# Cross-attention on one core: output products of two heads in one visit, with both heads' probabilities transposed first

## What is computed

```python
xn = (input - mu) * rsqrt(var + EPS) * gamma + beta
q  = Wq @ xn + bq                 # 8 heads x 64 channels
k, v = Wkv @ context + bkv
att = softmax(q^T k * 64**-0.5)   # 256 x 256 for each head and sample
y   = att @ v                     # heads concatenated
out = input + Wo @ y + bo
```

## Time and profile before

| | before |
|---|---|
| median of 3 runs | 944.0 us (943.9 to 944.01) |
| span of the profiled execution | 941.7 us |
| TensorE matmul busy | 919.0 us, 98% |
| VectorE busy | 810.3 us, 86% |
| ScalarE busy | 758.3 us, 81% |
| GpSimd busy | 671.0 us, 71% |
| mean granted TensorE clock | 0.999 |

### The profile page before, as it was taken

One profiled execution on the slowest core, in us unless ns is written; L12 is line 12 of the kernel. 1 busy time (PEld: TensorE's weight loads), 2 busy tenths in 40 slices (PEclk: granted clock), 3 DMA queues, 4 the chain that ended last, 5 costly groups with the idle time before them and its releaser, 6 DMA issues.

```text
span 941.7 us, 25082 instructions
## 1 busy us (share of the span) xinstructions
PE 919.0 (98%) x6852; PEld 691.6 (73%) x6852; DVE 810.3 (86%) x1899; ACT 758.3 (81%) x2569; POOL 671.0 (71%) x648
## 2 busy tenths in 40 slices
PE   5999999999999999999999999999999999999998
PEld 4777777777777777777777777777777777777775
DVE  5888889888889888898888898888898888898885
ACT  2788888788888878887888887888888888888785
POOL 2667777667787667877777776677776677777674
PEclk9999999999999999999999999999999999999999
DMA  6444444444444344444444444434444444433431
GB/s 120 100 107 95 114 100 100 96 106 93 107 110 95 91 109 100 95 117 94 95 100 106 100 105 97 104 89 115 103 100 93 106 96 103 114 90 83 96 82 36
DMA packets 72741, 93.32 MB, mean 99 GB/s; under 512 B 15316, under 2 KB 39892, under 8 KB 72724
## 3 DMA queue, kind: packets, MB, share of 16 engines
q1 hardware_dynamic: 70800, 92.72, 42.6%
q10 hardware_dynamic: 1924, 0.40, 0.3%
HBM read 21.76 MB, written 4.19 MB: 28 GB/s over the span
## 4 chain that ended last, share of the span: by engine, by line
PE 53%; DVE 24%; issue 13%; ACT 9%; DMA 0%; DVEq 0%; ACTq 0%; SPq 0%; POOL 0%
PE turned L488 15%; PE out_bank L502 14%; ACT probs L595 8%; PE fill L457 7%; PE fill L458 7%; DVE xhat L722 5%; DVE neg_max L676 5%; DVE probs_t L671 4%; PE misc L518 3%; PE misc L519 3%; DVE c_straight L730 2%; DVE c_crossed L731 2%; PE fill L463 2%; PE fill L464 2%; DVE t_low L687 2%
## 5 line engine op out<-in xcount | busy, mean ns | idle before, releaser
L788 POOL TENSOR_TENSOR probs<-probs,recip 128x512 f32<-128x512 f32 x512 | 526.6, 1055 | 155.6 <-DVE recip L682 150.0
L595 ACT ACTIVATE probs<-fill,neg_max 128x256 f32<-128x256 f32 x1024 | 475.4, 484 | 82.5 <-DVE neg_max L676 82.5
L676 DVE TENSOR_REDUCE neg_max<-fill 128x2 f32<-128x512 f32 x512 | 347.9, 680 | 65.4 <-PE fill L458 60.7
L488 PE MATMUL turned<-ident,probs 128*128 128x128 f32 x2048 | 325.5, 282 | 6.2 <-DVE probs_t L671 6.2
L457 PE MATMUL fill<-c_straight,t_stack 128*128 128x256 f32 x1024 | 308.9, 324 | 0.5 <-DMA t_stack<-t_low 0.5
L488 PEld LDWEIGHTS turned<-ident,probs 128*128 128x128 f32 x2048 | 224.0, 142 | 114.9 <-issue 62.6
L502 PE MATMUL out_bank<-probs_t,values 128*64 128x256 f32 x2048 | 277.5, 392 | 1.4 <-ACT probs_t L586 1.4
L458 PE MATMUL fill<-c_crossed,t_stack 128*128 128x256 f32 x1024 | 265.2, 280 | 0.0
L595 ACT ACTIVATION_READ_ACCUMULATOR probs<-fill,neg_max 128x1 f32 x1024 | 218.8, 214 | 0.0
L586 ACT COPY probs_t<-turned 128x512 f32<-128x512 f32 x256 | 150.1, 586 | 78.2 <-PE turned L488 77.9
L502 PEld LDWEIGHTS out_bank<-probs_t,values 128*64 128x64 f32 x2048 | 124.4, 136 | 105.7 <-issue 34.8
(11 more groups left out here) (61 smaller groups left out, 547.7 us busy)
## 6 DMA issues: line engine op xcount, KB each, us to landing
t_stack<-t_up SPq DMA_DIRECT2D x256, 128.0 KB, 2.3
t_stack<-t_low SPq DMA_DIRECT2D x256, 128.0 KB, 2.3
x<-in_x SPq DMA_DIRECT2D x64, 128.0 KB, 2.7
c<-in_ctx SPq DMA_DIRECT2D x64, 128.0 KB, 2.7
x_res<-in_x SPq DMA_DIRECT2D x32, 128.0 KB, 2.1
out<-y SPq DMA_DIRECT2D x32, 128.0 KB, 1.7
wq<-in_L_xattn_Wq ACTq DMA_DIRECT2D x2, 128.0 KB
wv<-in_L_xattn_Wkv SPq DMA_DIRECT2D x2, 128.0 KB
```

What stands on the lines that cost most here:

```text
L488: mm = pe.transpose(turned[unit % PT_BANKS][:, S * kt + 128 * qt:S * kt + 128 * qt + 128], probs[:, unit % PROBS, qt, 128 * kt:128 * kt + ...
L595: ins = act.activation(probs[:, unit % PROBS, qt, :], bank[:, K * qt:K * qt + K], ACT.Exp, bias=neg_max[:, unit, qt:qt + 1], accum_out=den ...
L676: dve.tensor_reduce(neg_max[:, unit, :], fill[bank_of("scores", unit)][:, :].rearrange("p (t k) -> p t k", t=QT), AX.X, ALU.max, negate=Tr ...
L788: pool.tensor_tensor(p, p, recip[:, unit, :].unsqueeze(2).broadcast_to([128, QT, K]), ALU.mult).then_inc(probs_ready, 1)
```

## The change

The visits of `attend` go from eight for a pair, one head each, to four, two heads each. Visit hp does heads 2hp and 2hp+1, waits for the copies of the last two of its four units, and is due at 6.1 + 4 hp, where the second head of the two was due before. `attended` is still raised once for each head. The number of matmuls, their operands and their order within the sum are as before.

With it three other works get a later due time, each by two steps: `result` on VectorE (18.63 to 20.63, so 2.63 to 4.63 modulo 16), `store` on SyncE (3.63 to 5.63) and `residual` on SyncE (8.5 to 10.5).

```diff
 PE_ORDER = (every("scores", -3.69, UNITS) + every("proj", PROJ, HP, 4) + every("turn", 1.26, UNITS)
-            + every("attend", 4.1, H, PS) + every("values", VALUES, PS * KT, DISTANCE)
+            + every("attend", 6.1, HP, 2 * PS) + every("values", VALUES, PS * KT, DISTANCE)
...
-                (-12.47, "sample_var", 0), (-11.46, "norm", 0), (-7.73, "c_hi", 0), (18.63, "result", 0)])
+                (-12.47, "sample_var", 0), (-11.46, "norm", 0), (-7.73, "c_hi", 0), (20.63, "result", 0)])
...
-              + [(-11.46 + 1.0, "load_x", 0), (-7.21 + 2.0, "load_c", 0), (8.5, "residual", 0),
-                 (18.63 + 1.0, "store", 0)])
+              + [(-11.46 + 1.0, "load_x", 0), (-7.21 + 2.0, "load_c", 0), (10.5, "residual", 0),
+                 (20.63 + 1.0, "store", 0)])
...
-            def attend(pair, h):
-
-                units = [PS * h + s for s in range(PS)]
-                for unit in units:
+            def attend(pair, hp):
+
+                for unit in (4 * hp + 2, 4 * hp + 3):
                     probs_t_wait(pe, pair, unit)
-                if h == 0:
+                if hp == 0:
                     wait(pe, values_ready, pair.count(PS * KT, PS * KT))
                     wait(pe, y_ready, pair.count(1, 0))
-                for kt in range(KT):
-                    for s in range(PS):
-                        mm = pe.matmul(out_bank[64 * s:64 * s + 64, 0:S], values[pair.parity()][:, s, kt, h, :],
-                                       probs_t[:, units[s] % PROBS_T, kt, :],
-                                       start=(h == 0 and kt == 0), stop=(h == H - 1 and kt == KT - 1))
-                mm.then_inc(attended, 1)
+                for h in (2 * hp, 2 * hp + 1):
+                    for kt in range(KT):
+                        for s in range(PS):
+                            mm = pe.matmul(out_bank[64 * s:64 * s + 64, 0:S], values[pair.parity()][:, s, kt, h, :],
+                                           probs_t[:, (PS * h + s) % PROBS_T, kt, :],
+                                           start=(h == 0 and kt == 0), stop=(h == H - 1 and kt == KT - 1))
+                    mm.then_inc(attended, 1)
```

## The result

The changed kernel takes 1009.9 us (median of 4 runs, 1008.5 to 1010.3) against 943.95 before: 1.070 times as long, interval 1.068 to 1.071. The direction was forecast, the size was not: 974 was expected, at most 985.

The account below looks back on a forecast made before the run. TensorE was taken to bound T10 to S6, VectorE S6 to the next T10. Span 941.7 + 44.4 (late result) - 13.3 (merges) - 1.2 (last pair) = 971.6, plus 2.3 gives 974 us; range 963 to 985.

Parts of the forecast that it names:

- What bounds the kernel: Each pair has two stretches: T10 to the next step's S6 bounded by TensorE, S6 to the next T10 by VectorE.
- What a merge saves: Each merged visit saves TensorE 0.30 us; only A4/A5 and A6/A7 count, 0.59 less losses, so 0.43 a pair.
- 0.1 at T11 and 0.05 at T12: Part of the 0.59 us merge saving lost at T11 and T12, to the semaphore and weights that can't be loaded ahead.
- What the moved result costs: Result queued behind norm on VectorE makes A01 wait, TensorE stands 2.4 us, T10 comes 1.48 us later, 30 times: +44.4.
- the 2.3 us of the sum: Amount by which the median of the runs lies above the traced span of 941.7, added to 971.6 to give 974.
- the last pair: It has no norm beside it and saves four merges: -1.2 us in the sum.
- rival 1: TensorE's clock falls to 1.2 GHz behind each stop, double visit takes 1.88 us more, 30 times: 1030; chance 0.07.
- That the late result is harmless: VectorE finishes result before A01 needs it, so only the 0.43 us merge saving counts: 930; chance 0.05.
- that TensorE alone bounds the kernel: TensorE is the only bound, so four merges of 0.30 us count in all 32 pairs: 906; chance 0.01.
- That only VectorE's own 0.40 counts: TensorE and ScalarE absorb the stop, leaving 0.40 - 0.43 a pair: no change, 943; chance 0.03.
- The room of copy 5: Slack on ScalarE between T5's end and copy 5's start, less the signal: 0.6 us, against T5 moving by 2.15.

## Why the prediction was right and wrong

**What bounds the kernel.** Right. The two halves of the merges show it: 0.38 a pair in the stretch from T10 to S6, nothing in the other.

**What a merge saves.** Right. A double visit at full clock lasts 1.88, as worked out. T10 to S6 went from 14.26 to 13.81 in the changed kernel, 0.45 against 0.43, and to 13.90 with `result` in its old place. The parts were less exact than the sum: I had allowed 0.1 at T11 and 0.05 at T12, and in the changed kernel T11 lost 0.01 (T10 to T11 took 1.85, and 3.01 less a visit of 1.17 is 1.84) and T12 0.10 (T11 to T12 took 1.07 instead of 0.97).

**What the moved result costs.** The mechanism was right in each link: `result` behind `norm` (466.46, predicted offset 0.34 from x_stack's start, measured 0.35), A01 0.05 behind its end, a stop of 2.31 recorded against 2.4, T5 to T10 7.23 against 7.1 to 7.33. The net price of an undisturbed pair was 1.0 against 1.05. Without the clock the span of the changed kernel would have been 941.7 + 30 x 1.0 = 972, and the time, with the 2.3 us of the sum, 974, which is the forecast; with the stop filled it is 976. That this comes out to the microsecond is partly luck. For the last pair I had taken off 1.2 beside its 0.43, and it got only 0.27 shorter, since its A01 waits for `result` too (0.68 us); the smaller price of the other pairs makes up for it.

**The clock.** This is the step that failed: the sum put the clock behind the stop at nothing. I had it as rival 1, with a chance of 0.07 and a price of 1.88 in each of 30 pairs, 1030. It happened, in 23 of 30, at 1.6. The argument against it was that TensorE works without a pause for the other 27 us of each pair. That was no evidence: the kernel before has no stop of this length in its loop from which the clock could have been read, and the one row that bore on it, the 1.42 us in the second pair, was shorter by over 1 us (2.6 from start to start in the changed kernel) and stood alone. The row of the end spoke for a fall, and I gave it too little weight and read it too coarsely. The last visit of `attend` in that trace, and two stretches behind it (granted clock is the last figure but two):

```profile
937.83 1.08 PE L502 MATMUL out_bank<-probs_t,values 128*64 128x256 f32 x8 [0.77 <-ACT probs_t L586]
...
939.00:940.10 1.10, 0.00 (x0) 0.00 (x0) 0.43 (x1) 0.00 (x0) 0.00 (x0) 1.00 0.00 0
940.20:941.60 1.40, 0.00 (x0) 0.00 (x0) 0.00 (x0) 0.00 (x0) 0.00 (x0) 0.50 0.27 94
```

The matmuls end at 937.83 + 1.08 = 938.91, so already in the old trace the clock fell within 1.3 us of TensorE's coming to a stand, after a stop of 0.77 us just before: both are shorter than the 2.4 us of stop that I forecast. The Trainium skill, "TensorE: Matmul & The Clock Gate", section "HAM oscillation — how this bites in real kernels", describes the pattern with a fall in every iteration; the trace agrees in the kind, a low stretch behind a stop, and shows it in 23 of 30 iterations. A chance far above 0.07 was due, and the range should have reached to 1030.

**The other rivals.** That the late result is harmless, and that TensorE alone bounds the kernel (906), fell with the result and with the 931.8 us of the merge alone. That only VectorE's own 0.40 counts, 943, is the case of `result` in front of `norm`, which I priced as +0.40 - 0.43 and which measures 941.25. So the same edit would have ended about as forecast by that rival, had it placed `result` one place earlier. The room of copy 5 named there is 467.84 - 467.06 - 0.1 = 0.68, not 0.6, which changes nothing.

## What to carry to other kernels

When work is moved in an engine's strict order, look at what it now stands behind, and who waits for it, before counting what the moved or merged work saves: here the merge gained 12 us, and a 0.4 us operation queued behind 2.1 us of another, instead of in front of it, cost 69, more than half of it by the clock (23 x 1.6 = 37). A stop of the matrix engine can have a second price, the clock behind it, and where the trace of the old kernel holds no stop of that length, that price is unknown and belongs in the range. A saving on the busiest engine counts only in the stretches that end on it, and two timelines half a pair long are enough to tell which these are.

## What the runs showed of the hardware

- A stop of 2.3 us, once in 29.5 us of otherwise dense matmuls, lets the granted clock fall from 2.4 to 1.2 GHz behind 23 of 30 stops; in the kernel with only `result` moved, all 30 stops of 4.2 us and the one of 2.5 us did so, 18 of them for 6.8 us instead of 3.4. The 1.42 us from start to start early in the trace of before did not, nor did the 1.06 us that is left of the stop with 0.5 us of matmuls in it, in 27 of 30 pairs. Behind a fall the same 16 records take up to 3.46 us instead of 1.88.
- 12 superfluous matmuls in each stop made the kernel 33 us faster (1009.9 to 976.45), 8 of them 34 us (975.9, one run), 4 of them 30 us (979.7, one run).
- Entering and leaving a visit of 64-column tiles costs TensorE 0.30 us in all: the first pitch, the change on either side, and 0.06 on the four transposes behind it (0.41 to the next scores instead of 0.35).
